# Attention, second half: the gate as one product of ones with a weighted sum, and two operations of the combination on GpSimd

## The reference, cut to what matters

```python
out = jax.ops.segment_sum(msg, tgt, num_segments=n).reshape(n, HID)
x_r = h @ Wskip + bskip
beta = jax.nn.sigmoid(jnp.concatenate([out, x_r, out - x_r], axis=-1) @ Wbeta)
return beta * x_r + (1.0 - beta) * out
```

## Time and profile before

| | us |
|---|---|
| median of 3 runs | 2683.86 (2680.4 to 2684.52) |
| profiled execution | 2679.54, of which the span from first to last instruction is 2677.8 |
| attention layer 0, second half: from `weight` to the last statistics | 775.39 to 919.44 |
| attention layer 1, second half | 1570.33 to 1714.89 |
| busy, whole span: PE, DVE, ACT, POOL | 2133.3, 1708.6, 1374.2, 1293.6 |

### The profile page before, as it was taken

The page is one execution under the profiler, slowest core; times in us unless marked ns, Lnnn a source line. Parts: engine busy times, 40 slices in busy tenths (PEclk is TensorE's granted clock), DMA queues, the critical chain, the costliest instruction groups (busy, mean ns, idle before and its releaser), DMA issues. The chain is left out here.

```text
span 2677.8 us, 38819 instructions
## 1 busy us (share of the span) xinstructions
PE 2133.3 (80%) x7614; PEld 1191.9 (45%) x7614; DVE 1708.6 (64%) x4970; ACT 1374.2 (51%) x2609; POOL 1293.6 (48%) x1119
## 2 busy tenths in 40 slices
PE   1888888897879656788848879569999989399997
PEld 0444444442223233344423323247677767166665
DVE  3888888872169778677751179657777776355552
ACT  1777877781112144566622222147676765366662
POOL 4444444417730000445448700067777764567774
PEclk9988899997779878899978889769999999699998
DMA  4676777753323287899953313399999996344440
GB/s 136 210 235 225 222 225 224 227 194 105 91 57 93 72 288 256 321 369 371 383 165 85 81 43 91 94 263 298 301 294 303 296 302 190 106 103 112 113 116 22
DMA packets 309081, 514.10 MB, mean 192 GB/s; under 512 B 86165, under 2 KB 182100, under 8 KB 308827
## 3 DMA queue, kind: packets, MB, share of 16 engines
q1 hardware_dynamic: 259000, 479.60, 56.5%
q0 software_dynamic: 46400, 33.03, 5.9%
q10 hardware_dynamic: 3552, 0.13, 0.1%
HBM read 291.41 MB, written 221.80 MB: 192 GB/s over the span
## 5 line engine op out<-in xcount | busy, mean ns | idle before, releaser
L474 POOL DMA_INDIRECT first_x<-in_x,first_index x200 | 256.3, 1281 | 296.1 <-issue 286.7
L741 POOL DMA_INDIRECT second_entry<-node_map,second_si x100 | 135.2, 1352 | 289.5 <-issue 184.6
L338 ACT ACTIVATE first_xn<-first_x,first_nb,first_rstd 125x128 f32<-125x128 f32 x600 | 245.1, 485 | 35.0 <-DVE first_nb L518 35.0
L994 PE MATMUL last_psH<-last_g,W2a 128*128 128x500 f32 x400 | 200.0, 625 | 35.3 <-DVE last_hid L956 35.1
L576 PE MATMUL first_psZ<-first_h,gate_h 128*128 128x500 f32 x250 | 141.3, 649 | 82.1 <-DVE first_y L537 82.0
L1268 DVE SCALAR_TENSOR_TENSOR att_prod<-att_bank,bk,att_qs 128x500 f32<-128x500 f32 x50 | 37.0, 739 | 253.4 <-ACT att_qs L1235 253.4
L1003 PE MATMUL last_psO<-W2b,last_hid 128*125 128x128 f32 x1600 | 192.3, 274 | 0.0
L1027 POOL DMA_INDIRECT elast_x<-x_rows,elast_si x100 | 140.3, 1404 | 95.6 <-issue 86.0
L1003 PEld LDWEIGHTS last_psO<-W2b,last_hid 128*125 128x125 f32 x1600 | 184.2, 189 | 0.9 <-issue 0.9
L660 POOL TENSOR_TENSOR bn_rs<-bn_rs,power 128x1 f32<-128x1 f32 x2 | 1.2, 580 | 348.1 <-DVE bn_rs L650 348.1
L338 ACT ACTIVATE last_xn<-last_x,last_nb,last_rstd 125x128 f32<-125x128 f32 x400 | 164.0, 487 | 0.1
(11 more groups left out here) (261 smaller groups left out, 5353.0 us busy)
## 6 DMA issues: line engine op xcount, KB each, us to landing
hT<-first_h SPq DMA_DIRECT2D x100, 250.0 KB
yT<-first_y SPq DMA_DIRECT2D x100, 250.0 KB, 3.8
second_yin<-yT SPq DMA_DIRECT2D x50, 500.0 KB
second_hin<-hT SPq DMA_DIRECT2D x50, 500.0 KB
yT<-second_y SPq DMA_DIRECT2D x50, 500.0 KB
last_yin<-yT SPq DMA_DIRECT2D x50, 500.0 KB
first_x<-in_x SPq DMA_DIRECT2D x100, 224.0 KB
h_rows<-second_rows SPq DMA_DIRECT2D x50, 448.0 KB
```

What stands on the lines that cost most here:

```text
L338: last = act.activation(xn[:, j], x[:, j], ACT.Relu, bias=nb[:, j:j + 1], scale=rstd[:, j:j + 1])
L474: pool.indirect_dma_start(x[:, to % X, j], None, a["x"], bass.IndirectOffsetOnAxis(index[:, end, r % 2, j:j + 1], 0), bounds_check=NODES - ...
L741: pool.indirect_dma_start(entry[:, q], None, scratch.node_map, bass.IndirectOffsetOnAxis(si[:, q], 0), bounds_check=NODES - 1, oob_is_err= ...
L994: last = pe.matmul(psH[h][:, 0:CH], w.W2a[:, 0, h * 128:(h + 1) * 128], g[:, q % 2], start=True, stop=True)
```

## The change

The gate's argument is no longer added up by two products in PSUM. ScalarE makes hdg = gate_h[column] * hd (`gate_part`, two copies in the memory of `fwd` and `run`), VectorE makes u = gate_out[column] * o + hdg (`gate_input`, two copies in `bwd` and `ex`), and TensorE multiplies the 128 x 128 ones with u. The column of gate_h or gate_out is read as one factor for each partition, from SBUF. `skip` is one product instead of two and no longer waits for the sigmoid.

`sig * dx` and `dx + o` go from VectorE to GpSimd (`mix`), as two operations of 128 x 500 that each wait for the one before. VectorE's stages are put in another order: the rest of `combine` (yn and statistics) is two chunks behind and comes first in the step, then `weigh`, `total`, `gate_input` and `difference` (the former 1363) of the same chunk. `difference` waits for `skip` of the same chunk, which TensorE does in its next step, after the next chunk's `value` and `spread`. ones becomes a tile that lives as long as the program.

```diff
                 def skip(k):
                     pe.wait_ge(m.dx, made(k - 2))
+                    if k < 2:
+                        pe.wait_ge(m.weight, made(0))
+                    pe.matmul(psX[k % 2][:, 0:CH], w.Wskip[:, l], hd[:, k], start=True, stop=True).then_inc(m.xz, 1)
+
+                def gate(k):
+                    pe.wait_ge(m.u, made(k))
                     pe.wait_ge(m.sig, made(k - 2))
-                    pe.matmul(psX[k % 2][:, 0:CH], w.Wskip[:, l], hd[:, k], start=True, stop=True)
-                    pe.matmul(psZ[k % 2][:, 0:CH], w.gate_h[:, l], hd[:, k], start=True, stop=False).then_inc(m.xz, 1)
-
-                def gate(k):
-                    pe.wait_ge(m.o, made(k))
-                    pe.matmul(psZ[k % 2][:, 0:CH], w.gate_out[:, l], o[:, k % 2], start=False, stop=True).then_inc(m.gated, 1)
+                    pe.matmul(psZ[k % 2][:, 0:CH], w.ones[:], u[k % 2][:], start=True, stop=True).then_inc(m.gated, 1)
...
+                def mix(k):
+
+                    s = k % 2
+                    pool.wait_ge(m.sig, made(k))
+                    pool.wait_ge(m.dx, made(k))
+                    pool.tensor_tensor(dx[:, s], sig[:, s], dx[:, s], ALU.mult).then_inc(m.gx, 1)
+                    pool.wait_ge(m.gx, made(k))
+                    pool.tensor_tensor(dx[:, s], dx[:, s], o[:, s], ALU.add).then_inc(m.y, 1)
+
+                steps(C, [(0, mix)])
...
+                def gate_part(k):
+
+                    act.wait_ge(m.weight, made(0))
+                    act.wait_ge(m.u, made(k - 2))
+                    act.activation(hdg[k % 2][:], hd[:, k], ACT.Identity, scale=w.gate_h[:, l, 0:1]).then_inc(m.hdg, 1)
...
-                steps(C, [(0, value), (1, gate)])
+                steps(C, [(0, gate_part), (0, value), (1, gate)])
...
-                    dve.wait_ge(m.gated, made(k - 2))
+                    dve.wait_ge(m.y, made(k - 2))
                     dve.wait_ge(m.pv, made(k))
                     dve.wait_ge(m.o, made(k - 1))
                     dve.tensor_tensor_scan(o[:, s], run_cont[:, q, 0:CH], pv[:, s], o[:, 1 - s, CH - 1:CH] if k else 0.0,
                                            ALU.mult, ALU.add).then_inc(m.o, 1)
...
+                def gate_input(k):
+
+                    s = k % 2
+                    dve.wait_ge(m.o, made(k))
+                    dve.wait_ge(m.hdg, made(k))
+                    dve.wait_ge(m.gated, made(k - 2))
+                    dve.scalar_tensor_tensor(out=u[s][:], in0=o[:, s], scalar=w.gate_out[:, l, 0:1], in1=hdg[s][:],
+                                             op0=ALU.mult, op1=ALU.add).then_inc(m.u, 1)
+
+                def difference(k):
+
+                    s = k % 2
                     dve.wait_ge(m.xz, made(k))
                     dve.wait_ge(m.o, made(k))
+                    dve.wait_ge(m.yn, made(k - 2))
                     dve.scalar_tensor_tensor(out=dx[:, s], in0=psX[s][:, 0:CH], scalar=w.bskip[:, l:l + 1], in1=o[:, s],
                                              op0=ALU.add, op1=ALU.subtract).then_inc(m.dx, 1)
-                    dve.wait_ge(m.sig, made(k))
-                    dve.wait_ge(m.dx, made(k))
-                    dve.tensor_tensor(dx[:, s], sig[:, s], dx[:, s], ALU.mult).then_inc(m.gx, 1)
-                    dve.wait_ge(m.gx, made(k))
-                    dve.tensor_tensor(dx[:, s], dx[:, s], o[:, s], ALU.add).then_inc(m.y, 1)
...
-                steps(C, [(0, weigh), (0, total), (1, combine)])
+                steps(C, [(2, combine), (0, weigh), (0, total), (0, gate_input), (0, difference)])
```

More of the change, by code:

```diff
@@ L176, in prepare @@
         w2u = ph.sb("w2u", [128, 256])
-        ones = ph.sb("ones", [128, D])
+        ones = w.ones
         win = ph.sb("win", [ECHUNK, CH + 2], I32)
@@ L1082, in attention @@
         yn = ph.sb("yn", [128, U, CH])
+        hdg, u = (fwd, run), (bwd, ex)
         bank = [ph.ps(f"bank{i}") for i in range(8)]
@@ L1095, in attention @@
         yn_stored = ph.stored("yn_stored", U)
-        names = "scattered xT hs qk qs prod score weight spread v vs pv o xz gated sig dx gx y yn ystats"
+        names = "scattered xT hs qk qs prod score weight spread v vs pv o xz gated hdg u sig dx gx y yn ystats"
         m = Group(**{n: ph.stage(n + "_made") for n in names.split()})
@@ L1356, in total @@
                                            ALU.mult, ALU.add).then_inc(m.o, 1)
+                def gate_input(k):
[7 more added lines that the diff above has]
+                    s = k % 2
+                    dve.wait_ge(m.xz, made(k))
+                    dve.wait_ge(m.o, made(k))
+                    dve.wait_ge(m.yn, made(k - 2))
+                    dve.scalar_tensor_tensor(out=dx[:, s], in0=psX[s][:, 0:CH], scalar=w.bskip[:, l:l + 1], in1=o[:, s],
+                                             op0=ALU.add, op1=ALU.subtract).then_inc(m.dx, 1)
                 def combine(k):
                     s, q = k % 2, k % U
[L1361 to L1364, removed]
-                    dve.wait_ge(m.sig, made(k))
-                    dve.wait_ge(m.dx, made(k))
-                    dve.tensor_tensor(dx[:, s], sig[:, s], dx[:, s], ALU.mult).then_inc(m.gx, 1)
-                    dve.wait_ge(m.gx, made(k))
-                    dve.tensor_tensor(dx[:, s], dx[:, s], o[:, s], ALU.add).then_inc(m.y, 1)
                     dve.wait_ge(m.y, made(k))
@@ L1746, in program @@
             Wskip=sb("Wskip", [128, L, D]), We=sb("We", [1, L, D]), gate_h=sb("gate_h", [128, L, D]),
[L1747 removed]
+            gate_out=sb("gate_out", [128, L, D]), heads=sb("heads", [128, D + 32]), blocks=sb("blocks", [128, D]), ones=sb("ones", [128, D]), ident=sb("ident", [128, 128]),
             W1a=sb("W1a", [128, 2, 256]), W1b=sb("W1b", [128, 2, D]), W2a=sb("W2a", [128, 2, 256]),
```

## The result

| | before | changed |
|---|---|---|
| median, 20 runs each (us) | 2681.44 (2672.55 to 2692.97) | 2698.23 (2683.97 to 2713.65) |
| profiled execution | 2679.54 | 2694.21 |
| second half, layer 0 (weights made to last statistics) | 144.05 | 151.35 |
| second half, layer 1 | 144.56 | 151.18 |

The ratio is 1.0065, 95% interval 1.0049 to 1.0081: the changed kernel is slower, by 13 to 22 us. The forecast was +20.6, a time of 2705 in 2695 to 2735. Of the 14.7 us between the two profiled executions 13.9 lie in the two second halves; the rest of the program together kept its length to 1 us, but not part by part: 1.5 us less ahead of the first second half, 3.1 less between the two, 5.3 more behind the second. Over the ten traces of this document these three stretches range over 7, 11 and 16 us, although no edit touches their work; that is enough to account for the scatter of whole executions.

A forecast was written before the change was run, and what follows sets the result against it. VectorE's step of 5.594 us was taken to bound the second halves; start +1.5, 22 steps at 5.97 +8.3 and end +0.5 make +10.3 a layer, +20.6 for two, so about 2705, range 2695 to 2735.

The forecast's parts named there:

- The bound: Second halves before the change: VectorE sets the step at 5.59 us, TensorE's 5.42 leaves it 0.17 to spare.
- The work without interference: Changed second halves: VectorE's six operations take 4.77 us a step, 4.85 when coupled with TensorE.
- the coupling: VectorE's difference waits for TensorE's skip, 4.84 us from u; two steps last 4.84 + 4.85, so 4.85 each.
- The exclusion: Second halves: VectorE operations with two SBUF inputs and GpSimd operations lock each other out for a whole instruction.
- The new step: Second halves: scan, sum, gate_input, gate, sigmoid and product form a closed chain of 5.97 us; bounds 5.85 to 6.2.
- The signs named: Second halves: scans near 1.6 us, gate_inputs 1.7, GpSimd's sum 2.2, its product 1.24; TensorE idle 1.3 before each gate.
- The start: Start of each second half: difference(0) waits for the skip, so scan(1) starts later, +1.5 us a layer.
- The end: After the last scan of each second half: 7.58 us instead of 7.11, +0.5 a layer.
- No exclusion: Rival: GpSimd's and VectorE's operations overlap freely in the second halves; step 4.85 us, both layers −32, 2652; chance 0.08.
- an unheld scan: Rival: scan not held, or VectorE goes ahead of a waiting GpSimd; step 5.06 us, both layers −20, 2664; chance 0.11.
- A gain that just pays for the loss: Rival: the change gives as much as it takes; step 5.5 to 5.6 us, 2679 to 2689; chance 0.03.
- The clock: Rival: TensorE's granted clock falls to 0.81 in the second halves, +15 us a layer on top, 2735; chance 0.07.

The follow-up runs named there:

- e2: Changed kernel with the gate as two products in PSUM again, GpSimd keeping its product and sum; ratio to before 0.9971, step 5.42 us.
- e7: e4 with difference one chunk behind, between combine and weigh; median 2648.52 us, ratio to before 0.9878, step 4.77 us.
- e6: Changed kernel with GpSimd's product and sum on 4 columns instead of 500, output incomplete; step 4.90 us on average.
- e4: e3 with pv in PSUM too, weigh writing back to the bank it read; one execution 2664.73 us, step 4.90 us.
- e3: Changed kernel with hdg written to PSUM, so gate_input reads one SBUF tensor and one from PSUM; ratio to before 0.9912, step 5.02 us.
- e5: Changed kernel with GpSimd's sum on the first 250 of 500 columns, output incomplete; step 5.29 us instead of 5.82.
- e7b: Changed kernel with difference one chunk behind, between combine and weigh, hdg and pv staying in SBUF; step 5.95 us.
- e1: Changed kernel with GpSimd's product and sum back on VectorE, leaving the new gate alone; one execution 2701.14 us, step 6.19 us.

## Why the prediction was right, point by point

- **The bound.** VectorE's 5.59 a step with TensorE's 5.42 close behind. e2 takes VectorE's load away and lands on 5.42.
- **The work without interference.** Worked out 4.77 for VectorE and 4.85 coupled; e7 shows 4.77, e6 and e4 4.90. The term for the coupling was 0.05 a step low, or 0.10 for two steps: the path from the end of gate_input to difference is 4.94 (866.44 to 871.38 in e6's rows), not 4.84. The 0.10 us that TensorE takes longer for a gate on which it had to wait (1.10 against 1.00) was seen in the row and left out of the sum.
- **The exclusion.** Taken from an addition in another phase and carried to a scan and to an operation with a factor for each partition, for which no row stood. Shown by e3 and e4, one operand at a time, and by e5 with half the dose. Who waits gets it in the order in which they came: scan before sum, sum before gate_input, in every steady step. The starts in a trace show the order only down to about 0.06 us: in e2, layer 1, the scan starts at 1584.95, 0.05 ahead of GpSimd's product, and yet is the one that is held (2.33, the product 1.23).
- **The new step.** Forecast 5.97, measured 5.82. This is the term that was mis-sized, and the three handovers take 0.20 less: scan 1.05 behind the product (taken 1.12), sum 1.04 behind the scan (1.10), gate_input 0.53 behind the sum (0.60). The product, in turn, starts 1.95 behind gate_input's end and not 1.91 (884.39 to 886.34). I took it that each waiting operation has 0.14 of its own time behind it when the other ends, as the addition has; the scan and gate_input have 0.21. That this is because they read a start value or a factor for each partition is my guess. GpSimd has 0.20 behind it after a scan, which is all that its operation on 4 columns takes in e6, but 0.14 after gate_input (the sum of 784.37 in layer 0 ends at 785.93, gate_input at 784.83) and 0.15 after the addition of the earlier trace rows. So an operation is not held for its whole length, as the prediction puts it, but for about the part that runs over the columns; what decides the last 0.06 is open. The signs named were near 1.6, 1.7 and 2.2 for scan, gate_input and sum and 1.3 of idle time ahead of the gate; measured were 1.52, 1.53, 2.01 and 0.97.
- **The start.** Taken as +1.5. To the end of the scan of chunk 2 it is 790.40 − 773.87 = 16.53, against 13.87: +2.7. The mechanism, `difference(0)` that waits for the skip, was right, but the operations of the first chunks collide as well, and the scan of chunk 2 takes 2.26. It starts at 788.14, 0.03 behind GpSimd's sum of 1.24, and is held by the whole of it; gate_input of that chunk then finds GpSimd idle and takes 0.74, so that the following step is shorter and 22 steps from there bring +4.3 instead of 22 × 0.23 = 5.0.
- **The end.** 7.49 behind the last scan against 7.11: +0.4, forecast +0.5. Start, steps and end make +7.3 in layer 0, measured +7.3 (151.35 − 144.05), forecast +10.3; layer 1 has +6.6.
- **What was costed at nothing** held: ScalarE's gate_part takes 0.70 and nobody waits for it (the sigmoid stands idle for 3.27 us of a step); weigh(0) still waits 2.13 us for spread(0); run_cont and the stores never show in a wait of VectorE.
- **The range.** The median of 2698.23 lies in 2695 to 2735, but under 2699, the lowest time that the prediction worked out from its bounds, and the step of 5.82 lies under their 5.85. Nothing in the prediction supports the 4 us from 2699 down to 2695. As a difference of medians, 16.8 us, the result stands inside the +15 to +31, as the 13.9 of the traces does not. The direction and the mechanism were right; that the time falls into the range owes something to luck.
- **The other phases** were to keep their length to 1 us. Their sum did (+0.7), but by −1.5, −3.1 and +5.3 that cancel. Such a sign can't be read from one trace of each kernel.
- **The rivals.** No exclusion (2652) and an unheld scan (2664) fell. The step worked out for the first, 4.85, is within 0.05 of e4's 4.90, where nothing is left to exclude. The 5.06 of the second has no run beside it: e3's 5.02 is near by chance, since it frees gate_input and not the scan. A gain that just pays for the loss (5.5 to 5.6 a step) fell with 5.82. The clock stayed at 1.00 in the steady part with TensorE busy 111.7 of 132.7 us.

## What to carry to other kernels

Before work goes from VectorE to GpSimd, mark which of VectorE's remaining operations have two tensors in SBUF: where the two meet and neither engine has time to spare, GpSimd's column time adds instead of hiding, above all when VectorE's operations depend on each other, since the waiting engine slips in between them. Where the one that is held has time to spare, as GpSimd in e2, it costs nothing. Often one operand is fresh from PSUM or can be left there; e3 moved one operand and turned +0.6% into −0.9%. Count an order change with the exclusion in it: the same order cost 0.13 us a step with it and won 0.13 without.

## What the runs showed of the hardware that I had not expected

VectorE can write its result back to the PSUM bank it reads and scan from there at no extra time: weigh 0.67 against 0.66, scan 1.25 against 1.26 (e4).

The start of a second half depends on when the clock comes back, and that differs even within one execution. TensorE has been idle for some 17 us when the weights are done. In the changed kernel its products are at the lower level for 3.5 us; in e2's layer 0 for over 9 us (windows of e2, columns as in the earlier trace rows), and that layer took 146.23 us where layer 1 took 141.95. The same shows in e6 (132.69 and 128.05) and e7b (158.79 and 155.20). Of the twenty second halves in the ten traces, ten are back at 1.00 within 3 to 5 us and ten after 8 to 12: both layers of e1, e3 and e7, layer 1 of e4, layer 0 of e2, e6 and e7b. Before and changed have the short form in both layers, so it is no part of the difference between their traces; the steps are not touched by it.

```profile
778.90:788.00 9.10, 9.07 (x10) 3.18 (x11) 1.88 (x2) 1.96 (x2) 0.00 (x0) 0.50 0.00 1
...
794.00:900.00 106.00, 106.00 (x237) 41.36 (x235) 74.18 (x97) 26.10 (x39) 67.00 (x39) 1.00 0.31 93
```

TensorE is busy all through both stretches; only the level differs. What decides between the two was not tried.
